# A mixture-of-experts stage in which ScalarE and GpSimd take one of eight weighted adds from VectorE

## The reference

```python
def _L1_ffn_ref(x, router_w, router_b, expert_w, expert_b):
    B, N, D, C, E, K = (8, 8192, 128, 128, 8, 2)
    router_probs = jax.nn.softmax(x @ router_w + router_b, axis=-1)
    top_p, top_i = jax.lax.top_k(router_probs, K)
    top_p = top_p / jnp.sum(top_p, axis=-1, keepdims=True)
    expert_out = jnp.einsum('bnd,edc->bnec', x, expert_w) + expert_b
    gathered = jnp.take_along_axis(expert_out, top_i[..., None], axis=2)
    return jnp.einsum('bnk,bnkc->bnc', top_p, gathered)
...
    t = t + _L1_ffn_ref(_ln_t(t), L1_ffn_router_w, L1_ffn_router_b, L1_ffn_expert_w, L1_ffn_expert_b)
    x = _from_tokens(t, x)
```

## Time and profile before

| what | us |
|---|---|
| three runs, median | 5550.67 |
| three runs, lowest and highest | 5549.47 and 5551.52 |
| the profiled execution | 5559.32 |
| its span in the trace | 5557.6 |
| busy in the span: PE | 4773.5 (86%) |
| busy in the span: DVE | 4864.6 (88%) |
| busy in the span: ACT | 4017.6 (72%) |
| busy in the span: POOL | 1610.2 (29%) |

### The profile page before, as it was taken

One profiled execution on the slowest core, in us unless ns is written; L12 is line 12 of the kernel. 1 busy time (PEld: TensorE's weight loads), 2 busy tenths in 40 slices (PEclk: granted clock), 3 DMA queues, 4 the chain that ended last, 5 costly groups with the idle time before them and its releaser, 6 DMA issues. The chain is left out here.

```text
span 5557.6 us, 100602 instructions
## 1 busy us (share of the span) xinstructions
PE 4773.5 (86%) x34168; PEld 1985.8 (36%) x34168; DVE 4864.6 (88%) x6244; ACT 4017.6 (72%) x5832; POOL 1610.2 (29%) x790
## 2 busy tenths in 40 slices
PE   5888879998778887999877887899987788789998
PEld 2333333334333333333433333333343333333334
DVE  6799779998789977999868997799986899689998
ACT  4787569994477757999447784799935778479993
POOL 1388700000048860000004885000000588500000
PEclk9899989999899998999988999899998899999998
DMA  1000030000000003000000000300000000030000
GB/s 41 0 1 0 16 66 10 10 6 24 24 0 1 0 16 66 10 10 6 24 24 0 1 0 16 66 10 10 6 23 24 1 1 0 16 66 10 10 6 31
DMA packets 42112, 89.63 MB, mean 16 GB/s; under 512 B 11595, under 2 KB 27798, under 8 KB 38550
## 3 DMA queue, kind: packets, MB, share of 16 engines
q1 hardware_dynamic: 41622, 83.21, 5.6%
HBM read 28.65 MB, written 8.39 MB: 7 GB/s over the span
## 5 line engine op out<-in xcount | busy, mean ns | idle before, releaser
L1576 ACT ACTIVATE arena<-ps 128x1024 f32<-128x1024 f32 x2048 | 1912.6, 1034 | 190.5 <-PE ps L1539 168.8
L1605 DVE TENSOR_TENSOR arena<-arena 128x1024 f32<-128x1024 f32 x1664 | 1899.6, 1216 | 17.8 <-ACT arena L1576 17.6
L1188 DVE TENSOR_TENSOR_SCAN arena<-ps,hlast,arena 128x512 f32<-128x512 f32 x1024 | 1251.5, 1265 | 28.3 <-ACT hlast L1070 13.9
L1133 POOL TENSOR_TENSOR arena<-arena 128x1024 f32<-128x1024 f32 x512 | 1201.6, 2357 | 240.2 <-ACT arena L1049 173.7
L1539 PE MATMUL ps<-arena 128*32 128x512 f16 x16384 | 1091.0, 382 | 111.2 <-issue 81.0
L1522 PE MATMUL ps<-arena 128*32 128x512 f32 x8192 | 1068.4, 600 | 7.3 <-ACT arena L1576 3.6
L955 PE MATMUL ps<-arena,ident 128*128 128x512 f32 x2048 | 964.8, 595 | 0.0
L1067 ACT ACTIVATE ps<-arena,amat 128x512 f32<-128x512 f32 x1024 | 704.5, 688 | 354.4 <-DVE arena L1188 345.4
L1539 PEld LDWEIGHTS ps<-arena 128*32 128x32 f16 x16384 | 464.6, 97 | 965.9 <-issue 667.8
L1911 POOL MEMSET arena<- 128x1024 f32 x4 | 3.8, 952 | 2452.5 <-POOLq L103 2452.5
L1164 DVE TENSOR_TENSOR arena<-arena,ps 128x1024 f32<-128x1024 f32 x416 | 497.4, 1196 | 80.9 <-PE ps L1024 80.9
(11 more groups left out here) (283 smaller groups left out, 4518.4 us busy)
## 6 DMA issues: line engine op xcount, KB each, us to landing
arena<-x SPq DMA_DIRECT2D x36, 512.0 KB, 5.2
arena<-arena SPq DMA_DIRECT2D x64, 256.0 KB, 6.0
arena<-arena SPq DMA_DIRECT2D x64, 224.0 KB, 5.8
arena<-arena SPq DMA_DIRECT2D x28, 512.0 KB, 3.7
arena<-pe SPq DMA_DIRECT2D x256, 32.0 KB, 1.8
out<-arena SPq DMA_DIRECT2D x8, 1024.0 KB, 3.9
expw<-L_ffn_expert_w SPq DMA_DIRECT2D x1, 512.0 KB
wqkv<-L_attn_W_qkv SPq DMA_DIRECT2D x1, 192.0 KB
```

What stands on the lines that cost most here:

```text
L1133: pool.tensor_tensor(halves(hb[s % RING]), halves(hb[s % RING]), cs[s % 4].unsqueeze(1).broadcast_to([128, HD, CH]), ALU.mult).then_inc(hc ...
L1188: dve.tensor_tensor_scan(halves(hb[s % RING])[:, h, :], da(s, h), halves(injected)[:, h, :], k.hlast[:, s, h, :], ALU.mult, ALU.add).then_ ...
L1576: act.activation(probs[p % 8], k.bank(2 * group[p], 2 * CH), ACT.Exp, scale=SCALE / SPLIT ** 2).then_inc(exp_s, 1)
L1605: dve.tensor_tensor(acc[p % 2], acc[p % 2], probs[p % 8], ALU.add).then_inc(acc_s, 1)
```

## The change

ScalarE and GpSimd take over the eighth expert (half 1, e = 3) of each tile:

- ACT multiplies that expert's 128 columns in PSUM by the gate into one of four SBUF buffers `weighed` (`weigh(i)`), as soon as both products of the tile are done and the buffer is free.
- POOL adds the buffer to the tile in `t1`, and raises `expert_added_early` (`pre_s`).
- DVE's first add of a tile (half 0, e = 0) now waits for that. It makes seven adds per tile: four of half 0, three of half 1. `added_by` counts accordingly, and PE's waits name the last of seven.
- ACT's stream is written by tiles: 32 `weigh`, among which the image copies, the mean (behind tile 13) and the variance (behind tile 21) stand.

```diff
             def experts(i):
                 for hb in range(2):
                     if i >= 3:
-                        pe.wait_ge(added, added_by(i - 3, hb, HE - 1))
+                        pe.wait_ge(added, added_by(i - 3, hb, HE - 1 - hb))
...
-                pe.wait_ge(added, added_by(i, 1, HE - 1))
+                pe.wait_ge(added, added_by(i, 1, HE - 2))
...
             moments = Chain(act, k.sem("moments"))
-            for g in range(NG):
-                if g == 3:
-                    channel_mean(k, act, moments, k.sem("x_in"), k.at(4096, L))
-                if g == 5:
-                    channel_variance(k, act, moments, k.at(4096, L))
+            act.wait_ge(gp, 1)
+
+            def weigh(i):
+                act.wait_ge(emm, 2 * i + 2)
+                if i >= 4:
+                    act.wait_ge(pre_s, i - 3)
+                act.activation(weighed[i % 4], k.bank(expert_bank(i, 1), C, (HE - 1) * C), ACT.Identity,
+                               scale=small["gate"][:, i, NE - 1:NE]).then_inc(w_s, 1)
+
+            def keep_image(g):
                 act.wait_ge(fm, g + 1)
...
+            for i in range(NT):
+                weigh(i)
+                if i == 13:
+                    channel_mean(k, act, moments, k.sem("x_in"), k.at(4096, L))
+                if i == 21:
+                    channel_variance(k, act, moments, k.at(4096, L))
+                if i % 4 == 3 and i >= 7:
+                    keep_image(i // 4 - 1)
+            keep_image(NG - 1)
+
         @block.gpsimd
         def _(pool):
             pool.memset(gpad, 0.0).then_inc(gz, 1)
+            for i in range(NT):
+                tile = t1[:, i * 128:(i + 1) * 128]
+                pool.wait_ge(w_s, i + 1)
+                pool.tensor_tensor(tile, tile, weighed[i % 4], ALU.add).then_inc(pre_s, 1)
...
                 tile = t1[:, i * 128:(i + 1) * 128]
+                if e == 0 and hb == 0:
+                    dve.wait_ge(pre_s, i + 1)
...
-                    if i >= 1:
+                    if i >= 1 and e < HE - 1:
                         add_expert(i - 1, 1, e)
```

More of the change, by code:

```diff
@@ L1800, in ffn @@
     HE, EXPERT_BANK, FINAL_BANK = NE // 2, 2, 0
+    weighed = [k.at(E0 + 4352 + i * C, C) for i in range(4)]
+    w_s, pre_s = k.sem("expert_weighed"), k.sem("expert_added_early")
     def expert_bank(i, hb):
@@ L1811, in added_by @@
             return e + 1
-        before = HE + NE * (step - 1)
-        return before + (e + 1 if step == NT else 2 * e + hb + 1)
+        before = HE + (NE - 1) * (step - 1)
+        if step == NT:
+            return before + e + 1
+        return before + (2 * e + hb + 1 if e < HE - 1 else NE - 1)
     def spread(col):
```

## The result

| what | before | after |
|---|---|---|
| median of the runs, us | 5551.10 (4 runs) | 5588.12 (4 runs) |
| lowest and highest, us | 5549.47 and 5557.28 | 5583.80 and 5592.95 |
| expert phase, end of the gate copy to the last add, four batches, us | 68.0, 68.0, 69.7, 69.65 | 76.1, 76.0, 76.25, 76.0 |
| their sum, us | 275.3 | 304.4 |

The change makes the kernel slower by the factor 1.0061 (95% interval 1.0046 to 1.0077), some 37 us. The forecast was 5574 with a range of 5558 to 5590: the sign and the range hold, the size is short: 37 us instead of 23.6. The new median lies 2 us inside the upper end of the range.

What follows compares the result with a forecast made beforehand. PE was taken as the bound in mid-phase, 2.163 us per tile against DVE's 2.07. Start 8.6, mean and variance 10.8 and end 4.2 sum to 23.6 us, which on 5550.67 gives 5574, range 5558 to 5590.

Steps and rivals of the forecast that it cites:

- DVE's relief in mid-phase: Mid-phase: 128 fewer DVE adds, 33 us of DVE time, worth nothing since PE still needs 2.163 us per tile.
- the middle with the longer path: Mid-phase: waiting for weighing and POOL's add leaves 0.9 us slack, so PE stays at 2.163 us per tile; 0.
- start, four batches: Phase start: DVE starts 3.05 us later, PE rests 3.4 us, clock falls in all batches; 8.6 us more.
- mean and variance, four batches: On ACT ahead of the weighings of tiles 14 and 22: PE stalls 2.7 us per batch, 10.8 in all.
- end, four batches: Phase end: last add comes 1.06 us later behind the last products in each batch, 4.2 us in all.
- L: Time from the start of a tile's products to DVE's first add on it: 2.65 us; mid-phase holds to 3.55.
- The low stretch: Phase start: clock at 0.50 from 1.0 to 7.8 us behind the old first add, expected in all four batches.
- The deduction for overlap: Mean and variance: ACT's instructions overlap some 0.1 us at their ends, so stalls of 1.6 and 1.4 became 2.7.
- DVE as bound: Rival, mid-phase: PE's waits on DVE are real, each add saved wins 0.26 us; 5546 us, chance 0.05.
- The buffers cover: Rival: no clock fall, PE's three-tile lead absorbs mean and variance to all but 1 us per batch; 5563, chance 0.11.
- The long path: Rival: POOL's add takes 1.16 us or waits for DVE's accesses, 13.8 us more; 5588 us, chance 0.12.

Runs made afterwards that it cites:

- seven adds alone: Kernel before with each tile's eighth add taken out and nothing in its place: 5553.09 us, ratio 0.9993.
- two more adds: Changed kernel with two extra unused 128-column adds on POOL ahead of each real one: 5602.95 us, ratio 1.0093.
- without mean and variance: Changed kernel with the channel mean and variance on ACT left out of the expert phase: 5575.13 us, ratio 1.0037.
- the mended kernel: Changed kernel with tiles 0 to 2 added by DVE alone, expert 0 weighed instead, mean and variance in four pieces each: 5554.34 us, ratio 1.0003.
- the second comparison: Changed kernel without any edit, run once more beside the kernel before on one chip: 5590.88 us, ratio 1.0064.
- the last kernel: The mended kernel plus a lighter PE final (one-pass transpose, bf16 bias product), gates' copy behind the first weighing: 5541.91 us, ratio 0.9975 against the kernel before.

## Why the prediction was right, and where it fell short

| step of the prediction | predicted, us | measured, us | from |
|---|---|---|---|
| DVE's relief in mid-phase | 0 | 0 | tiles 2.163 us apart; seven adds alone |
| the middle with the longer path | 0 | 0 | same; limit found with two more adds |
| start, four batches | 8.6 | 10.15 | last products without mean and variance against before |
| mean and variance, four batches | 10.8 | 13.5 | phase of the changed kernel, with and without them |
| end, four batches | 4.2 | 5.4 | last products to last add, 1.35 each |
| sum | 23.6 | 29.1 | phase 304.4 against 275.3 |

**The bound.** The step that all others rest on, that PE's free pace and not DVE's busy share limits the middle, is borne out from both sides: seven adds without a path change no tile's distance, and eight adds become the limit as soon as PE has less to do. What the prediction did not say is how near DVE stands: over a whole phase its adds alone need 67.0 of the 68.0 us. The 42.0 us that PE "waited for DVE" gave nothing back when DVE's work was shortened.

**The term that was mis-sized is L**, taken as 2.65 and measured as 2.85. The weighing was right (0.38 taken, 0.367 measured). POOL's add was taken in proportion to the larger ones of the earlier trace rows, at 0.30 us. The two lines of the changed kernel (duration ns, min/median/max, of all 128):

```profile
L1934 POOL TENSOR_TENSOR arena<-arena x128: 451/453/464, 1345.1 to 5572.3; 128x128 f32<-128x128 f32 x128
```

```profile
L1910 ACT ACTIVATE arena<-ps,arena x128: 359/367/379, 1344.6 to 5571.8; 128x128 f32<-128x128 f32 x128
```

It takes 0.453 us, so the proportion of 512 to 1024 columns does not hold at 128. The line through the two rows of large adds showed no fixed part, and two such rows can't exclude one. The other 0.06 us are hand-overs: the three of the path, at 1357.15 above, sum to 0.15 us instead of 0.09. L stands in 16 places, the start, two stalls and the end of four batches, so 0.2 us of it make some 3 of the 5.5 us by which the sum is short.

**Start.** The order of events was as predicted: weighing of tile 0 behind the copy of the gates, a rest of PE of 3.5 us (3.4 predicted), the fall of the clock in all four batches. DVE starts 3.29 us later than the old first add in the mean of the four batches, instead of 3.05 (in the first batch POOL's add 0.15, and the gates' transposes 0.12 later than taken), and tile 5 comes 10.4 to 10.6 us behind it instead of 10.1. The low stretch was put at 1.0 to 7.8 us behind the old first add, after the third batch of the earlier trace rows; it lay from about 4.7 to 8.2, where PE works again. The two misplacements nearly cancel, since PE stood still in the first part of the supposed stretch anyway.

**Mean and variance.** 1.6 and 1.4 us were predicted and then cut to 2.7 together, for overlaps of ACT's instructions. Measured by tile distances they take 3.93 - 2.163 = 1.77 (from 1376.62 to 1380.55 above) and 3.79 - 2.163 = 1.63 (at the variance), 3.4 together: the uncut numbers, each plus the 0.2 that L was longer. The deduction for overlap was the error.

**End.** 1.35 instead of 1.06 each: again 0.2 of L, and 0.06 in DVE's last ten adds, which take 3.12 us instead of 3.06.

**What stays open.** The medians differ by 37.0 and 35.1 us in the two comparisons, the phases of the traces by 29.1 and 29.0. The lower ends of the two intervals (1.0046 and 1.0051, 26 and 28 us) admit that the other 6 to 8 us are none. The change adds no work outside the phase, and no run isolates them. The traces show two things that make such differences without the change. Outside the four phases the span is 5273 to 5288 us in the ten traces, and it goes with the time that the granted clock stands at 0.50 there: 552 us in the shortest (the mended kernel), 602 and 605 in two of the longest. And a phase of the kernel before is 1.7 us longer in a batch that falls to the low clock. Its trace has two such batches, those of the five other kernels in which DVE starts right behind the gates one or none; in the changed kernel all four fall. What share of the 6 to 8 us these have is not shown.

**The rivals.** DVE as bound is refuted. The buffers cover nothing of the mean. The long path gave a time of 5588 us, which is the measured one, but not the mechanism: it wanted an add of 1.16 us and L of 3.5, and the add takes 0.453. That its time came out is chance. The kernel with L beyond that value took 5603. In part the range, too, held by luck: its upper end, 5590, came from this rival, and in the second comparison the changed kernel took 5590.88, beside 5555.74 for the kernel before.

## What to carry to other kernels

Before work is moved off a busy engine, compare start-to-start distances at free pace of it and of its neighbour: two engines at 2.07 and 2.163 us per tile are both the bound, and the gain appears only when both get lighter, as the last kernel shows. The relief of one engine is worth at most what the other's work leaves free over the whole phase, here 1.0 of 68.0 us, and not its slack per tile times the tiles. An instruction handed to another engine's queue inherits what stands ahead of it there (here a mean of 4 us and the copy of the gates); long steps in that queue should be cut in pieces before it becomes part of a tile's path. A small operation is not a large one scaled down: with no row of its size, the range has to hold a fixed part.

## What the runs showed of the hardware

- **Small adds on POOL.** 128 fp32 columns take 0.453 us in the changed kernel, where each add waits for its weighing. Back to back, in the kernel with two more adds, they start 0.36 us apart (two from 1366.74 to 1367.46). 1024 columns take 2.357, 0.295 per 128.
- **A bf16 product ahead of fp32 ones.** Four expert products take 1.94 us in the fastest kernel, behind the bf16 bias product, and 1.88 behind an fp32 one, where no bank is waited for. The 0.06 us lie at the first product: the second starts 0.485 us behind it instead of 0.429. The one-pass transpose and the bf16 bias product together shorten a tile by 2.163 - 1.937 = 0.23 us, with the 0.06 already paid.
- **The stretch from a batch's last add to the next scan** has the same work in each batch, yet takes 183 to 188 us. Windows of the kernel before, columns as above:

```profile
1412.70:1595.80 183.10, 134.51 (x389) 64.80 (x389) 127.81 (x241) 107.34 (x152) 1.93 (x9) 0.89 0.07 18
...
4169.10:4356.90 187.80, 137.90 (x389) 65.59 (x389) 127.79 (x241) 107.24 (x152) 1.93 (x9) 0.85 0.06 18
```

  The granted clock is 0.89 in the one and 0.85 in the other, with equal counts on every engine. PE is busy 3.4 us longer in the second, DVE and ACT are not.
